# Six waits of GpSimd on TensorE's semaphores, between its scattered row sends

## The reference

```python
x = x + layernorm(attn(layernorm(x)))       # recurrent block
x = x + layernorm(ffn(layernorm(x)))        # mixture of experts

# attn: ct = [previous token, token]; xv = sigmoid(relu(ct @ W_act.T)) read as complex numbers,
#       divided by the running maximum of their size; kv = their running product along the tokens
#       out = (kv @ W_val.T) * sigmoid(relu(ct @ W_rec.T)) ** 4

# ffn, per token: probs = softmax(x @ gate_w.T) over 64 experts; the 6 largest, normed to sum 1
#       routed = sum over the 6 of weight * (silu(x @ w1[e].T) @ w2[e].T)      inner width 176
#       shared = (silu(g) * u) @ shared_down.T, with g, u = x @ shared_gate_up.T
#       out = routed + shared
```

## Time and profile before

| | us |
|---|---|
| median of 3 runs | 299.45 |
| lowest and highest run | 294.72, 300.31 |
| the profiled execution | 300.68 |
| its span, first to last instruction | 298.9 |
| busy in the span: PE, DVE, POOL, ACT | 237.7, 176.2, 130.1, 80.9 |

### The profile page before, as it was taken

How to read it: one execution, slowest core, us unless ns; L and a number is a source line. 1 busy time by engine, 2 the same in 40 slices (tenths; PEclk the granted TensorE clock), 3 DMA queues, 4 the chain that set the end, 5 groups by cost and what they waited for, 6 DMA issues and landing times.

```text
span 298.9 us, 4224 instructions
## 1 busy us (share of the span) xinstructions
PE 237.7 (80%) x1382; PEld 178.2 (60%) x1382; DVE 176.2 (59%) x551; ACT 80.9 (27%) x184; POOL 130.1 (44%) x163
## 2 busy tenths in 40 slices
PE   6667959985486098674299989999999988998890
PEld 6333748552164086453277778888888766756480
DVE  3538896989997064580133797863454234424884
ACT  1484671383022104141002011111333302130032
POOL 6007500006777317477226643655565674553000
PEclk9997998999599679986579999999999997999996
DMA  7999999993323203245518999999988933567923
GB/s 234 361 372 372 368 380 420 420 416 142 121 100 118 79 0 119 71 157 195 166 37 279 301 339 341 363 309 406 326 293 272 328 130 99 171 222 256 367 80 105
DMA packets 34615, 72.00 MB, mean 241 GB/s; under 512 B 4576, under 2 KB 24608, under 8 KB 34080
## 3 DMA queue, kind: packets, MB, share of 16 engines
q1 hardware_dynamic: 29024, 55.68, 53.7%
q0 software_dynamic: 5568, 16.03, 14.3%
HBM read 44.89 MB, written 26.80 MB: 240 GB/s over the span
## 4 chain that ended last, share of the span: by engine, by line
issue 31%; PE 31%; DVE 14%; another core or an unknown queue 7%; DMA 7%; POOL 4%; SPq 3%; ACT 3%; ACTq 0%; DVEq 0%; POOLq 0%
PE bank L957 8%; PE bank L931 7%; PE bank L953 5%; PE bank L941 4%; PE bank L974 4%; SPq L380 3%; PE bank L751 2%; DMA early<-x_slots 2%; DVE work L1480 2%; DMA w_all<-y_rows 2%; DVE work L1407 2%; DMA y_rows<-zbuf,token_i 2%; DVE stats L1086 1%; DMA x_sb<-x 1%
## 5 line engine op out<-in xcount | busy, mean ns | idle before, releaser
L591 POOL DMA_INDIRECT y_rows<-zbuf,token_i x66 | 64.3, 974 | 60.6 <-DVE zbuf L1423 46.0
L562 POOL DMA_INDIRECT x_slots<-rows,slot_i x48 | 47.7, 993 | 60.2 <-DVE slot_i L1238 45.8
L1423 DVE COPY zbuf<-bank 128x256 f32<-128x256 f32 x66 | 24.2, 418 | 54.5 <-PE bank L957 48.4
L931 PE MATMUL bank<-work,w_all 128*128 128x128 f32 x256 | 34.1, 282 | 13.0 <-DVE work L1407 11.0
L706 ACT ACTIVATE sgu_sb<-bank 128x256 f32<-128x256 f32 x33 | 12.6, 383 | 105.8 <-remote 67.2
L931 PEld LDWEIGHTS bank<-work,w_all 128*128 128x128 f32 x256 | 31.4, 196 | 14.6 <-issue 14.5
L957 PE MATMUL bank<-w_all,sgu_sb 128*128 128x256 f32 x128 | 35.4, 413 | 0.0
L1407 DVE COPY work<-bank 128x512 f32<-128x512 f32 x33 | 22.5, 683 | 16.3 <-remote 15.0
L795 PE MATMUL bank<-x2nT,sgu_sb 128*128 128x256 f32 (+3 forms) x72 | 25.2, 503 | 7.4 <-issue 7.4
L957 PEld LDWEIGHTS bank<-w_all,sgu_sb 128*128 128x128 f32 x128 | 23.5, 198 | 10.4 <-issue 7.9
L795 PEld LDWEIGHTS bank<-x2nT,sgu_sb 128*128 128x128 f32 (+1 forms) x72 | 14.1, 205 | 15.4 <-issue 13.6
(11 more groups left out here) (214 smaller groups left out, 361.7 us busy)
## 6 DMA issues: line engine op xcount, KB each, us to landing
w_all<-pairs SPq DMA_DIRECT2D x32, 752.0 KB, 8.6
x_slots<-hidT SPq DMA_DIRECT2D x8, 1152.0 KB, 12.9
early<-x_slots SPq DMA_DIRECT2D x64, 144.0 KB
w_all<-y_rows SPq DMA_DIRECT2D x4, 1024.0 KB, 5.7
w_all<-y_rows SPq DMA_DIRECT2D x4, 512.0 KB, 8.8
y_rows<-zbuf,token_i POOLq DMA_INDIRECT x66
x_sb<-x SPq DMA_DIRECT2D x4, 256.0 KB, 4.0
out<-work SPq DMA_DIRECT2D x4, 256.0 KB, 2.1
```

The lines of the kernel that those rows point to most:

```text
L562: return pool.indirect_dma_start(x_slots, bass.IndirectOffsetOnAxis(ap=slot_i[:, c, k:k + 1], axis=0), rows[:, c, :], None)
L591: pool.indirect_dma_start(y_rows, bass.IndirectOffsetOnAxis(ap=token_i[:, s % 32:s % 32 + 1].bitcast(U32), axis=0), yS[:, s % 8, :], None) ...
L931: pe.matmul(h_b[t % 2][:, P * i:P * i + P], w[:, PK * k + P * i:PK * k + P * i + P], xT[:, t % 4, i, k, :], start=(k == 0), stop=(k == KC ...
L1423: dve.tensor_copy(yS[:, s % 8, :], y_b[s % 4][:, 0:C]).then_inc(y_done, 1)
```

## The change

GpSimd gets seven instructions that wait, six places in its two lists of sends, each for a count of a semaphore that TensorE raises. Nothing else is touched: no send is added, taken away or put in another order.

```diff
             for n in range(TOPK * TB):
+                if n == 15:
+                    pool.wait_ge(v_ps, 4)
+                elif n == 21:
+                    pool.wait_ge(x2T_ps, 4)
                 if n >= 3:
                     pool.wait_ge(sent_first[n % 3], 16 * (n // 3))
                 send(TOPK - 1 - n // TB, n % TB).then_inc(sent_first[n % 3], 16)
             pool.wait_ge(slot_done, 2)
             for n, (k, c) in enumerate(SECOND):
-                if n == 8:
+                if n == 7:
+                    pool.wait_ge(rank_ps, 3)
+                elif n == 8:
                     pool.wait_ge(slot_done, 3)
+                elif n == 13:
+                    pool.wait_ge(count_ps, 1)
+                elif n == 16:
+                    pool.wait_ge(tx_ps, 1)
+                elif n == 20:
+                    pool.wait_ge(h_ps, 1)
+                    pool.wait_ge(tx_ps, 2)
                 if n >= 3:
                     pool.wait_ge(sent_second[n % 3], 16 * (n // 3))
                 send(k, c).then_inc(sent_second[n % 3], 16)
```

## The result

The changed kernel takes 286.02 us (median of 4 runs, 285.86 to 289.37), the kernel before 299.25. The forecast was 288.0, with a range of 283.5 to 297.5.

A forecast was written before the change was run, and what follows sets the result against it. The prediction took TensorE's updates, held during long bursts of GpSimd sends, to bound the kernel. Gains of 4.2 (send 21), 7.2 (send 20) and 1.0 (clock) sum to 12.4 us: 300.68 - 12.4 = 288.3, taken as 288, range 283.5 to 297.5.

The forecast's parts named there:

- The bound: Before the even expert loop: long bursts of GpSimd sends hold TensorE's updates, so readers see them late, up to 8 to 9 us.
- The lag: Held updates pass some time after a burst's last send: 0.8 us for 4 sends, 1.5 for 7, 2.2 for 11.
- Send 15 and send 13: Waits for `v_ps` 4 (first list) and `count_ps` 1 (second list), expected already met: no pause, 0 us.
- Send 21: First list, wait for unit 2's transposes (`x2T_ps` 4): their copy comes at 99.35 in place of 103.56, 4.2 us gained.
- Send 7: Second list, wait for `rank_ps` 3: update passes at 121.0 in place of 122.47, 1.45 us for VectorE, 1.2 for the sends.
- Send 16: Second list, wait for `tx_ps` 1: first copy of loaded rows 0.8 us earlier, the other 0.6 of the 1.45 given back.
- Send 20: Second list, waits for `h_ps` 1 and `tx_ps` 2: second copy at 139.4 in place of 146.64, 7.2 us including 0.8.
- Clock: TensorE's work behind the two shortened holds runs at a higher clock: 1.0 us gained, between 0 and 5.2.
- The hold moves on: Rival: last sends and first four scatters form one burst holding pairs 1 and 2; 292.2 us, to 296; chance 0.12.
- Pauses free nothing: Rival: the delay has another cause, updates arrive as late as before, sends wait beside them; 300 us, no change; chance 0.14.
- the slower case: Rival: pauses free nothing, and displaced sends 21 to 23 and 20 to 23 hold others; 305 to 307.5 us; chance 0.07.
- the second rival: The rival "Pauses free nothing": updates arrive as late as before, 300 us, no change; chance 0.14.

The follow-up runs named there:

- e2: Changed kernel with only the waits before send 20 of the second list, all others taken out: 295.05 us, ratio 0.9885.
- e3: Changed kernel with only the two waits of the first list left: 297.89 us, ratio 0.9884.
- e6: All six waits of the changed kernel replaced by GpSimd waiting at sends 21, 7, 16, 20 for its own last send to land: 293.5 us.
- e13: Kernel before, with the first list's sends reordered and six GpSimd memsets after send 14: 302.37 us against 303.25.
- e12: Changed kernel unaltered, a third time, on another chip where the kernel before takes 275.78 us: 276.74 us, ratio 0.996.
- e7: Changed kernel unaltered, run again on the chip of e4 and e6: 286.89 us, ratio 0.9661.
- e1: Changed kernel with each wait moved to a semaphore of VectorE or ScalarE, the readers of TensorE's updates: 288.58 us, ratio 0.966.
- e4: Changed kernel without its waits at send 15 (`v_ps` 4) and the second list's send 13 (`count_ps` 1): 290.58 us, ratio 0.9828.

## Why the prediction was right, point by point

**The bound.** Right: the missing time was TensorE's updates, held by bursts of sends. e2, e3 and e6 show it by pauses alone, e13 by GpSimd's other work. What the kernel's profile could not show is that this holds on some chips only. That the pair was measured on one of them was luck: on the chip of e12 the ratio is 0.996, and nothing in the profile that was read gave a sign of it.

**The lag.** Taken as 2.2 us for 11 sends. For the very update that it stood for, unit 2's, e7 has 1.96 us and e1 2.03; down(0)'s update passes 2.06 to 2.08 us after send 20 in the changed kernel, e3, e4 and e6, but no profile with the short break lacks a pause there, so that the pause ended this hold isn't shown. For 7 sends 1.5; measured 1.41 in the changed kernel and 1.38 in e7. The number of sends doesn't fix it: it is 1.7 us after the 9 sends before send 16. And bursts don't hold all: in the kernel before down(0)'s update was seen 1.8 us after its matmuls ended, eight sends after the break, with sends going on.

**Send 15 and send 13, 0 us.** Right: gaps of 0.30, and e4 without them stands at 52.68 against 52.54.

**Send 21, 4.2 us.** Here a term was mis-sized. e7 gives nearly that (18.85 to 14.43, 4.4 us, with the forecast pause of 2.2 us and idle of 3). The execution profiled first gives 1.3. The step that I left out: an update held earlier in the same burst, `dn_ps` 1, has ScalarE's norms for unit 2 queued behind its reader. In the kernel before it passed at 92.86, in ScalarE's timeline:

```profile
92.86 0.60 ACT L646 ACTIVATE work<-bank 128x512 f32<-128x512 f32 x1 [2.20 <-remote]
```

The same profile has the break of 1.05 us at 83.08, which I had used only to count the burst. In the four profiles with a shorter break the wait at 21 comes too late, since the transposes themselves are late.

**Send 7, 1.45 us for VectorE.** Idle before its reader 2.59, forecast 2.7; pause 1.65, forecast 1.5.

**Send 16.** Pause 1.97, forecast 1. The update came at the upper bound, 1.73 us after send 15 ended, so more of send 7's gain was given back.

**Send 20, 7.2 us.** From unit 2's copy to the second copy the changed kernel takes 35.03 us and e7 36.07, against 43.08 before: 8.1 and 7.0 us. Idle before the second copy 4.25, forecast 4. The pause is 0.77, forecast 0.8, but not for the forecast's reason, a lag of 0.8 us behind send 19: the transposes end at 135.19 and VectorE's copy starts at 135.23, so nothing was held. The transposes themselves end 5.0 us after the first copy's start, and 4.15 in the kernel before, because the product ahead of them runs at the lower clock (2.05 us at 131.05, against 1.13 at 135.26 in the kernel before). The two differences about cancel, by luck.

**Together** 11.4 us were forecast up to the second copy. e7 has 11.4, the first profile 9.4. That the measured time is near the forecast 288 is in part luck too: in the first profile the 2 us that are missing up to the second copy are more than made up by 2.0 us ahead of all waits, and by 3.4 us behind the second copy, where 1.0 was forecast for the clock.

**Clock, 1.0 us.** Seen in one profile of two. From 130 to 142 us TensorE was granted 0.78 of full speed: its first product, after 3.23 us idle, still runs at the lower level (a granted 0.50, 2.05 us for eight matmuls at 131.05), the next at the upper (1.00, 1.13 us at 136.07). In the kernel before the stretch behind the hold was at 0.54. The windows of the changed kernel:

```profile
130.00:142.00 12.00, 10.08 (x60) 7.55 (x60) 1.65 (x5) 4.89 (x8) 7.66 (x8) 0.78 0.58 184
```

In e7 the same stretch (129.66 to 141.60) was granted 0.60, and the second product still ran at the lower level, after the same 0.88 us idle:

```profile
135.51 2.04 PE L944 MATMUL bank<-work,w_all 128*128 128x128 f32 x8 [0.88 <-issue]
```

The prediction's upper bound of 2.8 us for this stretch works out to 3.0 from its row (6.53 us of work at 0.54), which moves neither the sum nor the range.

Behind the second copy 3.4 us are won in the first profile and 1.6 in e7. Over the kernels on these chips that stretch takes 148.9 to 154.7 us, so I don't assign it.

**The rivals.** The hold moves on: not in the changed kernel, whose last sends and first scatters are 1.88 us apart (a wait of 3.28 us at 151.17, among its first scatters, answers to the 3.59 us at 160.84 in the kernel before), but seen in e6 (4.69 us). Pauses free nothing, and the slower case: refuted where updates are held. On the chip where none is held the outcome is that of the second rival, no change, and by a way that I had not thought of.

## What to carry to other kernels

If a reader is late although its matmuls have ended, lay the sends of GpSimd beside it. If the gap ends about 2 us behind a burst, put a pause in the burst just before the update that matters; here a wait on TensorE, on its readers or on GpSimd's own DMA served alike at the loop. Place it early enough for every held update that the critical one needs. The pauses of the changed kernel cost nothing that its profile shows, since nobody waited for the sends behind them; in e6 the displaced sends made a new hold. Then measure on a second chip before counting the gain: this one gave ratios of 0.9639 and 0.9661 where updates were held (the first pair and e7), and nothing on the chip of e12.

## What the runs showed of the hardware

- On three of the four chips whose runs are told apart here, an update that TensorE raised during a burst of GpSimd's indirect DMAs was seen up to 9.5 us late (e3), and then mostly 0.8 to 2.7 us after the burst (in e13 one passed within it, after 7.9 us). On the fourth, three profiles of changed kernels show none late, and the kernel before took 275.8 us in place of 299 to 303. What differs between the chips, and by which path a send holds an update, stays open.
- Memsets on GpSimd didn't hold updates (e13), but some of VectorE's instructions took longer beside them: its 128 x 256 norm (L1116 in e13) took 1.20 us, and 0.41 with no memset beside it. Others didn't: a 128 x 512 sum at 94.00 took 0.66 us, and 0.71 in the kernel before.

```profile
91.94 1.20 DVE L1116 TENSOR_SCALAR work<-work,mv,rstd 128x256 f32<-128x256 f32 x1
...
98.59 0.41 DVE L1116 TENSOR_SCALAR work<-work,mv,rstd 128x256 f32<-128x256 f32 x1
```

- A break of 1.04 us or more between sends went with an update raised some 8 us later that passed in the middle of the burst, one of 0.85 us or less with an update that didn't, in nine profiles. That the break is the cause was not tried by itself.
